# A recurrent mixer with routed experts: what the sync engine sends first, where decay factors are made, and when the last rows are fetched

## The reference, cut to what matters

```
x  = hidden_states                                   # 2 x 1024 tokens, 256 wide, float32
xn = layernorm(x)
proj = xn @ in_proj_w.T                              # gate 512, x 512, B 128, C 128, dt 64
xBC  = silu(conv_b + causal 4-tap conv(proj.xBC))
dt   = softplus(dt + dt_bias);  dA = dt * -exp(A_log)      # 64 heads of 8
y    = ssd(x * dt, dA, B, C) + D * x                 # linear recurrence along the 1024 tokens
hg   = y * silu(gate)
s    = hg * rsqrt(mean(hg^2) + 1e-5) * norm_w @ out_proj_w.T
e    = argmax(sigmoid(xn @ router_w)),  p = its probability
f    = p * ((silu(xn @ gate_w[e]) * (xn @ up_w[e])) @ down_w[e])    # 8 experts
out  = x + s * silu(f)
```

## Time and profile before

| | |
|---|---|
| three runs | 483.54, 484.0, 485.36 us; median 484.0 |
| profiled execution | 482.49 us, span from first to last instruction 480.4 us |
| busy PE / DVE / POOL / ACT | 396.6 / 325.6 / 216.2 / 192.1 us |
| mean granted clock of TensorE | 0.94 |

### The profile page before, as it was taken

One profiled execution on the slowest core, in us unless ns is written; L12 is line 12 of the kernel. 1 busy time (PEld: TensorE's weight loads), 2 busy tenths in 40 slices (PEclk: granted clock), 3 DMA queues, 4 the chain that ended last, 5 costly groups with the idle time before them and its releaser, 6 DMA issues. The chain is left out here.

```text
span 480.4 us, 7448 instructions
## 1 busy us (share of the span) xinstructions
PE 396.6 (83%) x2410; PEld 323.6 (67%) x2410; DVE 325.6 (68%) x691; ACT 192.1 (40%) x472; POOL 216.2 (45%) x252
## 2 busy tenths in 40 slices
PE   0885576187499999999999999999999999999650
PEld 0853234163478698978778977878778799998540
DVE  4535965264695676968949393968958385748778
ACT  1234847005326634355272734255162714252110
POOL 3200176268435081550827460550827184567820
PEclk9998769578799999999999999999999999999986
DMA  8930023661236175745364566646365566632794
GB/s 285 301 106 0 12 99 102 218 230 50 70 125 197 56 221 197 228 165 198 129 208 141 210 203 213 215 154 202 118 207 147 199 215 229 193 127 80 221 336 176
DMA packets 56470, 81.41 MB, mean 169 GB/s; under 512 B 5136, under 2 KB 34832, under 8 KB 56304
## 3 DMA queue, kind: packets, MB, share of 16 engines
q1 hardware_dynamic: 54560, 75.82, 49.1%
q0 software_dynamic: 1872, 5.13, 2.9%
HBM read 64.37 MB, written 16.56 MB: 168 GB/s over the span
## 5 line engine op out<-in xcount | busy, mean ns | idle before, releaser
L593 POOL TENSOR_TENSOR ARENA<-ARENA 128x512 f32<-128x512 f32 (+1 forms) x80 | 104.3, 1312 | 5.0
L1014 PEld LDWEIGHTS BANK<-ARENA 128*128 128x128 f32 x736 | 86.2, 194 | 14.0 <-ACT ARENA L846 7.2
L1014 PE MATMUL BANK<-ARENA 128*128 128x128 f32 x736 | 87.8, 278 | 7.9 <-ACT ARENA L846 6.9
L647 POOL DMA_INDIRECT gate_rows<-ARENA x23 | 22.8, 993 | 138.6 <-DVE ARENA L1271 81.4
L906 PE MATMUL BANK<-ARENA,W_MAIN 128*128 128x512 f32 x160 | 79.2, 643 | 5.6 <-DVE ARENA L1167 5.6
L1148 DVE SCALAR_TENSOR_TENSOR ARENA<-BANK,CONVC,ARENA 128x511 f32<-128x511 f32 (+2 forms) x72 | 53.7, 748 | 38.3 <-ACT ARENA L693 19.3
L1070 DVE TENSOR_TENSOR ARENA<-ARENA,BANK 128x256 f32<-128x256 f32 (+1 forms) x128 | 57.4, 449 | 12.5 <-POOL ARENA L661 7.3
L964 PE MATMUL BANK<-ARENA 128*128 128x128 f32 x384 | 49.2, 286 | 15.0 <-POOL ARENA L593 13.5
L1070 DVE TENSOR_TENSOR BANK<-BANK,ARENA 128x512 f32<-128x512 f32 (+1 forms) x80 | 50.3, 639 | 15.8 <-PE BANK L964 11.4
L906 PEld LDWEIGHTS BANK<-ARENA,W_MAIN 128*128 128x128 f32 x160 | 31.9, 209 | 40.5 <-issue 34.0
L964 PEld LDWEIGHTS BANK<-ARENA 128*128 128x128 f32 x384 | 46.4, 199 | 15.9 <-issue 14.2
(11 more groups left out here) (130 smaller groups left out, 630.0 us busy)
## 6 DMA issues: line engine op xcount, KB each, us to landing
ARENA<-source_rows SPq DMA_DIRECT2D x96, 144.0 KB, 3.0
ARENA<-in_w_gate SPq DMA_DIRECT2D x23, 512.0 KB, 3.7
ARENA<-in_w_up SPq DMA_DIRECT2D x23, 512.0 KB, 4.6
ARENA<-in_w_down SPq DMA_DIRECT2D x23, 512.0 KB, 5.2
source_rows<-ARENA SPq DMA_DIRECT2D x16, 288.0 KB, 2.7
ARENA<-in_x SPq DMA_DIRECT2D x8, 512.0 KB, 7.1
ARENA<-x_by_expert SPq DMA_DIRECT2D x23, 129.0 KB, 5.2
ARENA<-gate_rows SPq DMA_DIRECT2D x4, 512.0 KB, 8.5
```

Of the source, the lines that this page charges most:

```text
L593: nc.gpsimd.tensor_tensor(out=XS[par][rows, out_slot, 0:DIN].rearrange("p (a h) -> p a h", a=HD), in0=E2[par][rows, out_slot, :].unsqueeze ...
L647: pool.indirect_dma_start(out=g_dram, out_offset=bass.IndirectOffsetOnAxis(ap=TOKENS[:, t:t + 1], axis=0), in_=FY[par], in_offset=None).th ...
L1014: ins = nc.tensor.matmul(bank[:, f * P:(f + 1) * P], lhsT=WEXP[:, slot, at:at + P], rhs=FXT[par][:, j, :], start=(j == 0), stop=(j == DK - 1))
```

## The change

The step list changes in three places. `head t+1` comes ahead of `pair t+1`, which now stands behind the convolution blocks, `norm` and `flush` of that tile. The units are dealt out as 0, 1, 2, 2, 1, 2, 2, 1 and then seven times 2 (before: 0, 1, 1, eleven times 2, 1). On SP, `head 0` and `head 1` send their source rows ahead of the weights of units 0 and 1 and of the wait for the scatters. At the end, x and s of tiles 0 to 11 and x of tiles 12 to 15 (seven transfers of 512 KB) are fetched in the steps of tiles 12 to 14 into buffers that are free by then; ACT multiplies s by rnorm (12 instructions); only the four transfers of f are left behind `tail 13`, and `fin` is two DVE instructions of 1024 columns in place of five.

```
-UNITS = [0] + [1] * 2 + [2] * 11 + [1]
+UNITS = [0, 1, 2, 2, 1, 2, 2, 1, 2, 2, 2, 2, 2, 2, 2]
-TAIL_STEPS = {("tail", LAST - 1): [("rn", 0, 0)],
-              ("tail", LAST + 1): [("rn", 1, 0), *(("load", g, 0) for g in range(FIN + 1))],
-              ("sum", LAST + 3): [("fin", 0, 0), ("fin", 1, 0)],
+TAIL_STEPS = {("tail", LAST - 1): [("rn", 0, 0), ("bring", 0, 0), ("bring", 1, 0)],
+              ("head", LAST + 2): [("bring", 2, 0), ("bring", 3, 0)],
+              ("tail", LAST): [("bring", 4, 0), ("bring", 5, 0)],
+              ("head", LAST + 3): [("bring", 6, 0)],
+              ("tail", LAST + 1): [("rn", 1, 0), *(("scale", g, 0) for g in range(FIN)),
+                                   *(("load", g, 0) for g in range(FIN + 1))],
               ("tail", LAST + 2): [("rn", 2, 0)],
-              ("tail", LAST + 3): [("rn", 3, 0), ("fin", 2, 0), *(("last", LAST + c, 0) for c in range(GT))]}
+              ("sum", LAST + 3): [*(("fin", g, 0) for g in range(FIN)), *(("last", LAST + c, 0) for c in range(FIN))],
+              ("tail", LAST + 3): [("rn", 3, 0), ("last", LAST + FIN, 0)]}
@@ tile_steps
-        steps += [("pair", t + 1, 0)] * (u % 2) + [("head", t + 1, 0)]
+        steps.append(("head", t + 1, 0))
     steps += conv[:-1] * early + [("norm", t - 1, 0)] * (u > 0) + conv[-1:] * early
...
+    if ahead:
+        steps += [("pair", t + 1, 0)] * (u % 2)
     for unit in units[:1]:
@@ sp_step
                 if kind == "head" and t == 0:
-                    for k in range(1, FXN):
+                    sp.wait_ge(routed, 1)
+                    sp.wait_ge(scattered, 16 * TILES)
+                    for k in range(WSLOTS):
                         load_rows(k)
-                        if k < WSLOTS:
-                            load_gate_up(k)
-                            load_down(k)
+                if kind == "head" and t == 1:
+                    for k in range(WSLOTS):
+                        load_gate_up(k)
+                        load_down(k)
+                    for k in range(WSLOTS, FXN):
+                        load_rows(k)
...
+                if kind == "bring" and t <= FIN:
+                    if t == 0:
+                        sp.wait_ge(d_written, conv_of(GROUPS - 1, ORDER[-1]))
+                    rows = x_dram[:, t * GT:(t + 1) * GT, :]
+                    sp.dma_start(LX if t == FIN else ZX[t], rows).then_inc(x_back[t], 16)
+                if kind == "bring" and t > FIN:
+                    g = t - FIN - 1
+                    if g == 0:
+                        sp.wait_ge(hg_ready, LAST)
+                        for par in range(2):
+                            sp.wait_ge(o_stored[par], 16 * (LAST // 2))
+                    sp.dma_start(ZO[g], o_tiles[:, g * GT:(g + 1) * GT, :]).then_inc(o_back[g], 16)
+                if kind == "load":
+                    if t == 0:
                         for par in range(2):
                             sp.wait_ge(g_scattered[par], 16 * ((NT + 1 - par) // 2))
...
-            sp.wait_ge(routed, 1)
-            sp.wait_ge(scattered, 16 * TILES)
-            load_rows(0)
-            load_gate_up(0)
-            load_down(0)
             for s in STEPS[FIRST:]:
@@ act_step
+                if kind == "scale":
+                    act.wait_ge(o_back[t], 16)
+                    act.wait_ge(rn_ready, 1)
+                    for c in range(GT):
+                        of = t * GT + c
+                        ins = nc.scalar.activation(ZO[t][:, c, :], ZO[t][:, c, :], ACT.Copy, scale=RNORM[:, of:of + 1])
+                    ins.then_inc(o_scaled, 1)
@@ dve_step, fin
-                    for c in range(GT):
-                        of = t * GT + c
-                        ins = nc.vector.scalar_tensor_tensor(out=ZG[t][:, c, :], in0=ZO[t][:, c, :], scalar=RNORM[:, of:of + 1],
-                                                             in1=ZG[t][:, c, :], op0=ALU.mult, op1=ALU.mult)
-                    ins.then_inc(fin_chain, 1)
+                    tt(ZG[t], ZO[t], ZG[t], ALU.mult).then_inc(fin_chain, 1)
                     dve.wait_ge(fin_chain, t + 1)
                     tt(ZX[t], ZX[t], ZG[t], ALU.add).then_inc(fin_made, 1)
```

More of the change, by code:

```diff
@@ L125 @@
           "tx": (1, 0), "gu": (0, 2), "dn": (1, 0), "fy": (0, 0),
-          "sum": (0, 0), "rn": (0, 0), "load": (0, 0), "fin": (0, 0), "last": (0, 0)}
+          "sum": (0, 0), "rn": (0, 0), "bring": (0, 0), "scale": (0, 0), "load": (0, 0), "fin": (0, 0), "last": (0, 0)}
 ORDER = [HB + HB, HB + HB + 1, *range(HB, 2 * HB), *range(HB)]
@@ L268, in mixer_moe_kernel @@
         XBC, GATE = [], []
+        conv_at = place[0]
         for _ in range(2):
@@ L272, in mixer_moe_kernel @@
         conv_end = place[0]
+        CONV0_FLAT = ARENA[:, conv_at:(conv_at + conv_end) // 2]
         WEXP = part(WSLOTS * WE).rearrange("p (e c) -> p e c", e=WSLOTS)
@@ L337, in rows4 @@
             return flat[:, n * GT * DM:(n + 1) * GT * DM].rearrange("p (t d) -> p t d", d=DM)
-        FIN_FLAT = [XNT_FLAT, WEXP[:, 0, :], WEXP[:, 1, :]]
-        ZG, ZX, ZO = ([rows4(flat, n) for flat in FIN_FLAT] for n in range(3))
-        LG, LX = rows4(BC_FLAT, 0), rows4(BC_FLAT, 1)
+        ZX, ZO = ([rows4(flat, n) for n in range(FIN)] for flat in (XNT_FLAT, CONV0_FLAT))
+        LX, LG = (rows4(flat, FIN) for flat in (XNT_FLAT, CONV0_FLAT))
+        ZG = [rows4(CONV0_FLAT, FIN + 1), rows4(WEXP[:, 0, :], 0), rows4(WEXP[:, 1, :], 0)]
         BANKS = [ctx.enter_context(nc.psum_tensor(f"BANK{i}", [P, 512], FP32)) for i in range(RING_A + RING_D)]
@@ L373, in mixer_moe_kernel @@
         g_scattered = sems("g_scattered0 g_scattered1")
-        fin_loaded = [sem(f"fin_loaded{g}") for g in range(FIN + 1)]
+        x_back, o_back, g_back = ([sem(f"{n}_back{g}") for g in range(FIN + 1)] for n in "xog")
+        o_scaled = sem("o_scaled")
         fin_chain, fin_made, last_chain, last_made = sems("fin_chain fin_made last_chain last_made")
@@ L518, in sp_step @@
                         load_rows(t + FXN)
-                if kind == "load" and t < FIN:
-                    g, tiles = t, slice(t * GT, (t + 1) * GT)
-                    if g == 0:
+                if kind == "bring" and t <= FIN:
[3 more added lines that the diff above has]
+                    sp.dma_start(LX if t == FIN else ZX[t], rows).then_inc(x_back[t], 16)
@@ L523, in sp_step @@
                             sp.wait_ge(g_scattered[par], 16 * ((NT + 1 - par) // 2))
[L524 to L530, removed]
@@ L531, in sp_step @@
-                if kind == "fin" and t > 0:
-                    store_fin(t - 1)
+                    g = t
+                    rows = g_tiles[:, g * GT:(g + 1) * GT, :]
+                    sp.dma_start(LG if g == FIN else ZG[g], rows).then_inc(g_back[g], 16)
+                if kind == "last" and t == LAST:
+                    for g in range(FIN):
+                        store_fin(g)
                 if kind == "last":
-                    if t == LAST:
-                        store_fin(FIN - 1)
-                    else:
+                    if t > LAST:
@@ L1285, in dve_step @@
                 if kind == "fin":
-                    dve.wait_ge(fin_loaded[t], 16 * 3)
-                    dve.wait_ge(rn_ready, 1)
-                    for c in range(GT):
-                        of = t * GT + c
-                        ins = nc.vector.scalar_tensor_tensor(out=ZG[t][:, c, :], in0=ZO[t][:, c, :], scalar=RNORM[:, of:of + 1],
-                                                             in1=ZG[t][:, c, :], op0=ALU.mult, op1=ALU.mult)
-                    ins.then_inc(fin_chain, 1)
+                    dve.wait_ge(o_scaled, t + 1)
+                    dve.wait_ge(g_back[t], 16)
+                    dve.wait_ge(x_back[t], 16)
+                    tt(ZG[t], ZO[t], ZG[t], ALU.mult).then_inc(fin_chain, 1)
                     dve.wait_ge(fin_chain, t + 1)
@@ L1296, in dve_step @@
                     c = t - LAST
-                    dve.wait_ge(fin_loaded[FIN], 16 * 2)
+                    dve.wait_ge(g_back[FIN], 16)
+                    dve.wait_ge(x_back[FIN], 16)
                     dve.wait_ge(rn_ready, 2 + max(0, c - 1))
```

## The result

| | before | changed |
|---|---|---|
| median of four runs each | 484.59 us (483.54 to 485.36) | 469.68 us (468.74 to 471.04) |
| ratio, 95% interval | | 0.9718 [0.968, 0.9755] |
| profiled execution, span | 482.49, 480.4 us | 471.04, 469.2 us |
| busy PE / DVE / POOL / ACT | 396.6 / 325.6 / 216.2 / 192.1 us | 401.1 / 315.5 / 215.5 / 196.4 us |
| mean granted clock | 0.94 | 0.934 |

The forecast was 467.5 (462 to 475). Medians fell by 14.9 us, the spans of the two profiled executions by 11.2 only: that of the changed kernel is the slowest of its four runs, and that of before was faster than all four in the table. The steps read in these two profiles thus come out 3.7 us small in sum.

The account below looks back on a forecast made before the run. PE's work was taken to bound the kernel from 131 to 434 us, with chains across engines at both ends. Opening −13.6, units −5.5 + 2.4, end +0.3 sum to −16.4: 466.1 profiled, 467.5 median, range 462 to 475.

Parts of the forecast that it names:

- The bound and the mechanism: PE's work sets the time from 131 to 434 us; SP's rows behind weights delay POOL and PE's first unit.
- it doesn't do what it says: Rival: DVE and ACT's loop sets the pace behind 113 us, the earlier start is lost by tile 5: 479, chance 0.04.
- the opening gives less: Rival: scatters slow the store and fetch of tiles 0 and 1's rows, 6 to 7 us lost: 474, chance 0.12.
- The rows, 11.1: Opening: tile 0's rows stored and fetched ahead of the weights spare POOL its wait, 11.1 us gained.
- The order of the factors, 2.5: Opening, tile 1: decay factors behind the convolution let its taps start earlier, 2.5 us gained to PE's first unit.
- "Nothing, ±0.5 us" in the later odd tiles: Same swap in tiles 3, 9 and 11: earlier taps offset ACT's later tanh; taken as 0, bounds −3 and +3 for all.
- The units: New dealing: one unit less on PE by tile 13's end, −5.5; +2.4 back since `mid 5` comes only 3.1 earlier.
- The end: After tile 13: POOL and DVE 1.8 us late in tile 15, `fin` 1.5 shorter: +0.3, bounds −2 and +4.
- The collision: Rival, end: tile 15's rows or the last weights wait behind an early fetch: +4, 471.5, chance 0.10.
- The slower rival: If taps don't start earlier, ACT's tanh and PE are 4.2 us late in seven odd tiles: +29, 497, chance 0.04.

Follow-up runs that it names:

- e1: Kernel before with one edit only, source rows of tiles 0 and 1 ahead of the weights on SP: 468.8 us, ratio 0.9711.
- e2: Changed kernel with SP's opening as before, weights of units 0 and 1 ahead of the source rows: 477.46 us, ratio 0.9882.
- e3: Changed kernel with the decay factors ahead of `head` and the convolution again: 465.16 us, ratio 0.9668.
- e9: Kernel before with the source rows ahead of the weights and the new end; factors ahead of the convolution, old units: 466.53 us, ratio 0.967.
- e6: Changed kernel with the decay factors behind the first unit of a tile instead of ahead of it: 463.94 us, ratio 0.9607.
- e7: Changed kernel with the decay factors behind the first unit of a tile and units dealt as before: 463.42 us, ratio 0.9591.
- e10: Changed kernel with the decay factors behind `mid` of the tile before, just ahead of the step that uses them: 464.59 us, ratio 0.9607.
- e11: Changed kernel with the decay factors behind the first unit and ACT's twelve scalings behind `norm 14`: 463.74 us, ratio 0.9588.
- e8: Changed kernel with ACT's twelve scalings of the final rows moved behind `norm 14`: 468.49 us, ratio 0.9698.
- e4: Changed kernel with the units dealt as before: 469.66 us, ratio 0.9738.
- e5: Changed kernel with the old end: final rows all fetched behind the last scatter, no scaling on ACT: 471.19 us, ratio 0.9737.

## Why the prediction came out, step by step

The measured time is 2.2 us above the forecast, and the profiled execution 5 us above the 466.1 worked out for it. By landmarks: opening −11.7 (forecast −13.6), middle −1.1 (−3.1), end +1.6 (+0.3). The store of tile 0's rows comes 1.3 us later in this profile than the rows were written before; from the rows' being written on, the opening is −13.0 (51.8 and 38.8). That this is near the forecast is luck: two errors in it, of the rows and of the factors, nearly cancel.

- **The bound and the mechanism: right.** SP's order was the cause of POOL's wait, the wait of 11.10 us fell to 0.87 and 1.54 (0.32 in e1), and PE, full behind its first unit, ended earlier by about what it began earlier. e1 shows that this one edit carries the change; *it doesn't do what it says* and *the opening gives less* fall with it. Among the scatters the fetch of tile 0's rows followed their store after 2.14 us, as without weights ahead; that of tile 1's took 4.56 us (83.30 to 87.86), but POOL came to them at 94.33 and did not wait.
- **The rows, 11.1: mis-sized.** From the rows' being written to the first unit it was 51.8 us (42.5 + 9.3) and is 37.8 in e1: 14.0. I stopped at the first wait; tile 1's rows, behind unit 1's weights, had a wait of 4.04 us of their own on the way to the pair.
- **The order of the factors, 2.5: wrong for where they were put.** By its own rows the term should have been 2.1: 113.1 is when ACT's copy begins, and PE began 0.42 us after it (126.33 and 126.75). With the rows late the swap gives 3.0 (e2). Once the rows have taken that 4 us, the swap shortens the way to the taps by 3.1 us (28.2 in the mean of e1, e3 and e9, 25.1 in the mean of the eight where the factors come later), but the pair adds 4.1 ahead of the unit's copy. From store to unit it is 37.2 to 37.8 us with the factors first, 37.0 to 38.8 in the four kernels with them second: nothing. Behind the unit it is 33.6 to 35.3 (e6, e7, e10, e11): there the swap gives 2 to 4 us, and the opening as a whole 16.5 to 18.2, beyond the 15.4 that I had as its upper bound.
- **"Nothing, ±0.5 us" in the later odd tiles: the step that failed.** Tiles 5 and 9 stall by 2.25 + 0.68 and 1.28 + 0.67 us, and PE runs part of what follows at the lower clock. I had followed ACT to the unit's tanh and left out that the unit's turn needs a bank that ACT frees only with the pair. I had priced a loss of 2.4 in tile 5 and none in tile 9. The middle is 2.0 us longer than forecast, and 2.1 longer than with the factors first (e3).
- **The units: about right in size.** I had −5.5 + 2.4 in the middle and a part of the end's +1.8; the profiles have −3.0, −4.4 and −1.3 in the middle, and the times of three pairs show no gain.
- **The end: terms right, sum short.** The store of tile 15's rows is 1.3 us later against the end of `mid 13` (430.82 less 421.35, and 442.27 less 434.1), as forecast. From the store to POOL's first term it is 15.7 us instead of 14.1: 1.0 of it is the scatter, 0.7 the longer way of the rows. So DVE begins tile 15 2.9 late, not 1.8. `fin` and `last` are 10.7 instead of 12.0: −1.35 (forecast −1.5). The scalings are hidden, as said (0.77 us of cover left; e8, e11).
- **The collision: 0.7 us at most.** Two fetches of s were issued from 422.72 on and took 8.1 and 8.9 us to land, the second 1.5 us after the store of tile 15's rows at 430.82. From that store to POOL's product it took 7.2 us, 6.5 before. The 4 us that I had estimated by the Trainium skill's rule ("DMA: Bandwidth & Descriptors", section Issuing engines are not separate DMA queues) for a fetch still under way did not come. The last down weights, issued just ahead of the two fetches, did take longer to land, 7.2 us and not 3.7, but PE's last down product did not wait for them (429.99).
- **The slower rival** was right in that ACT is late for the unit, and wrong in its condition and price: the taps of tile 1 do start earlier, and it is three tiles and not seven, with 4.1, 2.9 and 2.0 us of its 29.

The swap as a whole costs 2.4 us by the ratios (3.3 with the old units); both pairs point the same way, with intervals that overlap. The landmarks of e3 and the changed kernel give more: from store to unit 1.4, middle 2.1, end 0.8. (Their spans differ by 6.5; the other 2.2 is the store itself, behind steps that are the same in both.) Of these the 1.4 lies inside the spread of kernels with one and the same opening. What stays open is what sets that spread, why the end differs by 0.8, and what the edits without the rows (e2) give alone, 2 or 6 us.

## What to carry to other kernels

Before pricing an order of transfers, follow the freed chain past the first wait: the same queue order may hold a second one behind it, and an edit meant for the second may then have nothing left to win. When a step is moved behind another, ask for every engine what stands next in its queue, and put the moved work behind the first thing that the bound engine waits for: here one line lower was worth 5 to 7 us, in three pairs.

## What was not expected of the hardware

In the eleven kernels with the rows ahead of the weights, the steps ahead of SP's store of tile 0's rows are the same, and yet it stands between 71.4 and 76.9 us. The granted clock from 60 to 75 us (ahead of the last two numbers of a row) goes with it: 0.89 where the store is at 71.4 (e9), 0.81 and 0.84 at 74.2 and 74.1 (e1, e3), 0.75 at 74.2 to 74.9 (e7, e10, e11), 0.56 to 0.63 at 75.5 to 76.9 (changed, e4, e5, e6, e8). The two rows are of e9 and of e8:

```profile
60.00:75.00 15.00, 10.74 (x51) 7.89 (x52) 6.28 (x16) 9.90 (x26) 11.55 (x15) 0.89 0.34 118
60.00:75.00 15.00, 11.43 (x30) 6.56 (x31) 8.52 (x17) 7.09 (x17) 11.64 (x12) 0.56 0.29 105
```

At 66 us the same twelve small matmuls take 1.60 us in e10 and 2.93 in the changed kernel and in e6. The opening of a single profile of this kernel can thus lie up to 5.5 us from that of another, more than most of the edits are worth. That the lower clock causes the later store, and what sets the clock there, is not shown.

In the changed kernel the granted clock fell from 1.00 (2.4 GHz) behind the short stalls of tiles 5 and 9, to a mean of 0.72 to 0.84 over the next 4 to 6 us. It stayed at 1.00 in e4, with 0.67 us of stall in tile 5, and in e10, with 1.33 and 0.96. But the size of the stall alone does not decide it. In e5 tile 5 stalls by the same 2.25 and 0.67 us as in the changed kernel and the clock stays at 1.00; in e11 a stall of 2.12 us leaves it at 1.00, where in e6 one of 2.09 is followed by a mean of 0.71 from 213 to 217 us. In e8 tile 9 stalls by 1.27 and 0.67 us, as in the changed kernel, and its eight down products take 2.00 us and not 3.65:

```profile
316.21 2.00 PE L1046 MATMUL BANK<-ARENA 128*128 128x256 f32 x8 [0.67 <-ACT ARENA L791]
```

So the clock's part in the price of such a stall differs from one execution to another, and one profile does not give it.
